# Where the positional product and the next step's value product stand in TensorE's queue: a fused attention and routed-expert block on one Trainium2 core

## What is computed

```python
h = _layernorm(x) * (1 + ca) + sa
q, k, v = jnp.einsum('bsx,xAnh->Abnsh', h, w)
a = jnp.einsum('bnqh,bnkh->bnqk', q + q_bias, k) * h ** (-0.5)
emb = jnp.einsum('sf,fnh->nsh', sins, positional * FREQS ** (-0.5))
a = a + relative_causal(jnp.einsum('bnqh,nvh->bnqv', q, emb) * h ** (-0.5))
a = softmax(where(mask, a, NEG_INF));  o = einsum(a, v);  x = x + ga * (o @ out_kernel + out_bias)
h = _layernorm(x) * (1 + cb) + sb
idx = argmax(softmax(h @ Wg + bg));  x = x + gb * gate * expert[idx](h)   # first 256 tokens of each expert
```

## Time and profile before

| what | value |
|---|---|
| median of three runs | 934.0 us |
| the profiled execution: its own time, its span | 934.63 us, 932.6 us |
| PE busy | 869.1 us, 93% of the span, 5515 matmuls |
| weight loads (PEld) | 684.8 us, 73% |
| DVE busy | 702.9 us, 75% |
| ACT busy | 704.5 us, 76% |
| POOL busy | 519.2 us, 56% |
| mean granted TensorE clock | 0.988 of full speed |

### The profile page before, as it was taken

The page is one execution under the profiler, slowest core; times in us unless marked ns, Lnnn a source line. Parts: engine busy times, 40 slices in busy tenths (PEclk is TensorE's granted clock), DMA queues, the critical chain, the costliest instruction groups (busy, mean ns, idle before and its releaser), DMA issues.

```text
span 932.6 us, 18151 instructions
## 1 busy us (share of the span) xinstructions
PE 869.1 (93%) x5515; PEld 684.8 (73%) x5515; DVE 702.9 (75%) x2115; ACT 704.5 (76%) x1971; POOL 519.2 (56%) x789
## 2 busy tenths in 40 slices
PE   7899999999999999999999999999999999998994
PEld 5666777767777777777776777777777777666994
DVE  4878778787878788777878787878877777843784
ACT  4688888878888888888887888888888888760551
POOL 3364545666556655665556655675566545543354
PEclk8999999999999999999999999999999999999998
DMA  7332221122100101011101110010101110105671
GB/s 286 92 91 61 85 84 52 46 56 60 44 24 18 54 22 44 24 41 40 32 24 36 36 43 24 21 38 20 44 24 35 33 38 18 32 9 197 224 217 40
DMA packets 36512, 56.01 MB, mean 60 GB/s; under 512 B 7446, under 2 KB 21511, under 8 KB 36160
## 3 DMA queue, kind: packets, MB, share of 16 engines
q1 hardware_dynamic: 32624, 46.16, 17.3%
q0 software_dynamic: 3072, 5.94, 1.8%
q10 hardware_dynamic: 720, 2.75, 0.8%
HBM read 23.96 MB, written 16.82 MB: 44 GB/s over the span
## 4 chain that ended last, share of the span: by engine, by line
PE 87%; issue 5%; DVE 2%; ACT 2%; DMA 1%; POOL 1%; SPq 0%; DVEq 0%; POOLq 0%; ACTq 0%
PE bank L837 23%; PE bank L867 15%; PE bank L847 15%; PE bank L804 13%; PE bank L823 5%; PE bank L874 4%; PE bank L834 3%; PE bank L1059 2%; PE bank L1048 2%; PE bank L1012 2%; ACT prob L611 1%; DMA kx<-in_ktab 1%; PE bank L895 1%; DVE klo L1207 1%; DMA x<-xbuf 1%
## 5 line engine op out<-in xcount | busy, mean ns | idle before, releaser
L451 POOL TENSOR_SCALAR prob<-prob,rsum 128x128 f32<-128x128 f32 (+3 forms) x512 | 263.7, 533 | 290.1 <-DVE rsum L1180 284.4
L611 ACT ACTIVATE prob<-srow,nmax 128x512 f32<-128x512 f32 (+3 forms) x512 | 287.0, 562 | 140.5 <-DVE nmax L1168 140.0
L1168 DVE CUSTOM_DVE_ANT_0 srow<-bank,consts 128x512 f32<-128x512 f32 (+3 forms) x512 | 246.4, 484 | 92.4 <-issue 52.2
L847 PE MATMUL bank<-consts,prob 128*128 128x128 f32 x1280 | 204.2, 274 | 0.2 <-POOL prob L451 0.2
L847 PEld LDWEIGHTS bank<-consts,prob 128*128 128x128 f32 x1280 | 155.1, 141 | 28.2 <-ACT pt L620 7.5
L837 PE MATMUL bank<-khi,qhi 128*128 128x512 f32 (+2 forms) x384 | 151.7, 395 | 18.8 <-issue 16.3
L867 PE MATMUL bank<-pt,v 128*64 128x512 f32 (+3 forms) x1024 | 151.9, 438 | 12.8 <-issue 10.8
L620 ACT ACTIVATE pt<-bank 128x384 f32<-128x384 f32 x318 | 151.6, 494 | 1.1 <-PE bank L847 1.0
L444 POOL TENSOR_TENSOR qlo<-qx,qhi 128x384 fp32r<-128x384 f32 x128 | 129.4, 1011 | 31.3 <-ACT qhi L579 31.3
L867 PEld LDWEIGHTS bank<-pt,v 128*64 128x64 f32 x1024 | 76.0, 136 | 84.0 <-issue 64.3
L837 PE MATMUL bank<-khi,qlo 128*128 128x512 f32 (+2 forms) x384 | 130.2, 339 | 0.0
(11 more groups left out here) (193 smaller groups left out, 1467.9 us busy)
## 6 DMA issues: line engine op xcount, KB each, us to landing
qx<-g SPq DMA_DIRECT2D x252, 64.0 KB, 2.0
xbuf<-fill SPq DMA_DIRECT2D x16, 385.0 KB, 4.2
x<-xbuf SPq DMA_DIRECT2D x16, 385.0 KB, 3.7
raw<-in_w SPq DMA_DIRECT2D x16, 256.0 KB, 3.3
prob<-in_w SPq DMA_DIRECT2D x16, 256.0 KB, 4.4
out<-row SPq DMA_DIRECT2D x8, 256.0 KB, 2.7
x<-in_x SPq DMA_DIRECT2D x1, 1792.0 KB, 15.0
modb<-mod_rows SPq DMA_DIRECT2D x8, 192.0 KB, 3.6
```

The source lines that it names most:

```text
L451: end = gp.tensor_scalar(part, part, rsum[:, par, 4 * h + q:4 * h + q + 1], 1.0, ALU.mult, ALU.mult)
L611: act.activation(prob[:, par, h, QOFF[q]:QOFF[q] + P * (q + 1)], srow[:, k % 4, 0:P * (q + 1)], ACT.Exp, bias=nmax[:, par, k:k + 1], scale ...
L847: last = pe.transpose(out[:, n * P:(n + 1) * P], prob[:, par, h, QOFF[q] + k * P:QOFF[q] + (k + 1) * P], ident)
L1168: dve.tensor_tensor_reduce(out=srow[:, k % 4, 0:w], in0=scb[k % 2][:, 0:w], in1=mask[:, S - w:S], scale=-1.0, scalar=BIG, op0=ALU.add, op1 ...
```

## The change

TensorE: `project_g` moves from k 6, ahead of the last scores, to k 7, behind them and ahead of `weighted`. The value projection of even steps moves from their k 1 to k 7 of the odd step before, also ahead of `weighted`; its waits for `x2`, `hh` and `prx` move with it, now in steps 1, 3 and 5. Odd steps keep their own value projection at k 1 and so have two. The wait for `hld` goes from each projection to the few places that need it, and the wait for the low keys of head 1 at k 4 goes, since `project_q` at k 3 has waited for them.

ScalarE: `evac_v` follows (at the end of odd steps, ahead of `evac_o`), and `evac_k(j + 1, 0)` goes ahead of `high_q(j + 1, 0)`. `second` stays where it is.

VectorE: in even steps `low_k(j + 1, 0)` comes first and `evac_g` behind it, with `recip` between its halves. `low` goes from k 7 to k 6 of step 4, `residual2` from k 7 to k 6 of step 1, `choice` from step 4 to k 1 of step 5, `route` and `index` from step 5 to k 1 and k 2 of step 6.

```diff
@@ scalar: step
-                    if before and k == 1 and not (last and V_OF[a][0]):
+                    if k == 1 and a % 2 and not (last and V_OF[a][0]):
                         evac_v(j + 4, prb[1], *V_OF[a][1:])
...
                     if after and k == 5:
+                        evac_k(j + 1, 0)
                         high_q(j + 1, 0)
-                        evac_k(j + 1, 0)
...
                 if after:
                     evac_k(j + 1, 1)
+                if a % 2 and v_after(j) is not None:
+                    evac_v(j + 5, prb[1], *v_after(j))
                 if before:
                     evac_o(j - 1)
@@ tensor: scores
-                    pe.wait_ge(s["kl"], 2 * j + h + 1)
+                    if k == 0 or j == NJ - 1:
+                        pe.wait_ge(s["kl"], 2 * j + h + 1)
@@ tensor: step
-                    if before and k == 1 and not (last and V_OF[a][0]):
-                        if a % 2:
-                            pe.wait_ge(s["gq"], j + 3)
-                        else:
-                            pe.wait_ge(s["ve"], j + 3)
-                            if a and not first:
-                                pe.wait_ge(s[(None, "x2", "hh", "prx")[a // 2]], b)
+                    if k == 1 and a % 2 and not (last and V_OF[a][0]):
+                        pe.wait_ge(s["gq"], j + 3)
...
-                    if k == 6 and a % 2 == 0 and j + 2 < NJ:
-                        pe.wait_ge(s["ve"], j + 4 if before else 1)
+                    if k == 7 and a % 2 == 0 and j + 2 < NJ:
                         if a == 2 and not last:
                             pe.wait_ge(s["hn"], b + 2)
-                        if a == 4 and not first:
+                        elif a == 4 and not first:
                             pe.wait_ge(s["lge"], b)
+                        else:
+                            pe.wait_ge(s["ve"], j + 4)
                         project_g(j // 2 + 1)
+                    if k == 7 and a % 2 and v_after(j) is not None:
+                        if first or a == 7:
+                            pe.wait_ge(s["ve"], j + 4)
+                        else:
+                            pe.wait_ge(s[("x2", "hh", "prx")[a // 2]], b)
+                        project_v(prb[1], *v_after(j))
@@ vector
-                if (a, k) == (4, 7):
+                if (a, k) == (4, 6):
                     low(n)
-                if (a, k) == (1, 7):
+                if (a, k) == (1, 6):
                     residual2(b)
-                if (a, k) == (4, 6):
+                if (a, k) == (5, 1):
                     choice(b)
-                if (a, k) == (5, 6):
+                if (a, k) == (6, 1):
                     route(b)
-                if (a, k) == (5, 7):
+                if (a, k) == (6, 2):
                     index(b)
...
-                    if k in (6, 7) and a % 2 == 0 and j + 2 < NJ:
-                        evac_g(j // 2 + 1, k - 6)
...
                 if after:
                     low_k(j + 1, 0)
+                places = a % 2 == 0 and j + 2 < NJ
+                if places:
+                    evac_g(j // 2 + 1, 0)
                 recip(j, par, 1)
+                if places:
+                    evac_g(j // 2 + 1, 1)
```

More of the change, by code:

```diff
@@ L240, in qraw, with v_after @@
             return qx[:, j % 2, h, :]
+        def v_after(j):
+            b, a = divmod(j + 1, PAIRS)
+            return None if b == B or b == B - 1 and V_OF[a][0] else V_OF[a][1:]
         def g_batch(c):
@@ L800, in project @@
                 else:
-                    pe.wait_ge(s["hld"], 2 * (n + 1))
                     hi, lo = (t[:, n % 2, :] for t in (hhi, hlo))
@@ L809, in project_q @@
                 pe.wait_ge(s["kl"], 2 * j)
+                if (n, a) == (0, 5):
+                    pe.wait_ge(s["hld"], 2)
                 project(prb[0][:, :], whi[:, a, 0:P], wlo[:, a, 0:P], n, "qp")
@@ L815, in project_g @@
             def project_g(c):
+                if c % NG == 0 and c:
+                    pe.wait_ge(s["hld"], 2 * (g_batch(c) + 1))
                 project(prb[1][:, :], gwhi[:, c % NG, :], gwlo[:, c % NG, :], g_batch(c), "tp")
```

## The result

| | before | after |
|---|---|---|
| median of 4 runs, us | 933.6 (933.0 to 934.8) | 983.2 (981.1 to 985.9) |
| profiled execution, us | 934.6 | 981.1 |
| its span, us | 932.6 | 979.1 |
| PE busy, us (matmuls) | 869.1 (5515) | 900.7 (5515) |

The changed kernel takes 1.053 times as long, with an interval of 1.050 to 1.056. Between the two profiled executions the difference is 46.5 us, between the medians 49.6. The forecast was 976 us, its range 961 to 986: sign and range held, and the forecast was 7 us too low.

What follows compares the result with a forecast made beforehand. TensorE's idle time was taken to bound the kernel. Step terms of +4.8 us a batch made 34 over seven batches, +1 for the first: 934.6 to 969.6; the clock's +7.5 gave 977, forecast as 976 us, range 961 to 986.

Steps and rivals of the forecast that it cites:

- The wait for `hh`: Step 3, k 7: the value product waits for ScalarE's `second`; TensorE idles 3.2 us, next step +3.5 us later.
- The rival in which these reads end in time: Shared bank's two reads end before TensorE reaches k 7: 927 us, chance 0.04; with late low queries 938 us, 0.03.
- The wait for `x2`: Step 1, k 7: the value product waits for `residual2` on VectorE; +1.3 us, about 1.1 us of it idle.
- Keys ahead of queries: ScalarE: `evac_k` first makes low queries 0.64 us later against 0.31 slack; steps 7, 0, 1, 3 +0.37 us, step 6 +0.15.
- the rival in which the low queries come in time: GpSimd's spans or ScalarE's order leave low queries in time: 1.3 us a batch less, 960 to 967 us, chance 0.12.
- Even steps free: Even steps losing their value product, some 0.7 us, become no shorter: `project_q` at k 3 waits for low keys anyway.
- The "0.5 to 0.6 us" of waiting: Sign expected in the profile after: `project_q` in even steps waits 0.5 to 0.6 us for `low_k`.
- the clock: Step 3's idle gap brings 1.2 GHz back: 1.6 us a fall, in two thirds of seven batches, +7.5 us (0 to +11).
- The rival in which the clock stays: Same waits but no fall to 1.2 GHz, since TensorE was fully busy around the gap: 969 us, chance 0.30.
- `choice`, `route` and `index`: VectorE: moved to steps 5 and 6, they delay these; +0.44 us for step 5, +0.85 for step 6, low queries included.
- Step 4: `low_k` first removes 1.35 us of waiting ahead of step 5, and the late `project_q` goes too: -1.7 us a batch.
- The sum: All eight steps: +4.8 us a batch, 34 over batches 1 to 7, +1 for the first batch, together +35 without the clock.

Runs made afterwards that it cites:

- e2_fill: The changed kernel with twelve thrown-away matmuls put ahead of the wait for `hh` in step 3: 967.8 us, ratio 1.0358 to the kernel before.
- e11_kfirst: The kernel before with only `evac_k` put ahead of `high_q` on ScalarE: 949.7 us, ratio 1.0144.
- e3_qfirst: The changed kernel with `high_q` ahead of `evac_k` again on ScalarE: 975.2 us, ratio 1.0447 to the kernel before.
- e4_vector: The kernel before with only the new VectorE order: 921.1 us, ratio 0.9874.
- e8_alone: The kernel before with only the value product of step 4 moved to k 7 of step 3, behind the wait for `hh`: 972.8 us, ratio 1.0402.
- e7_keepall_qfirst: The changed kernel with all even steps' value products back at k 1 and `high_q` ahead of `evac_k` again: 925.8 us, ratio 0.9880 to the kernel before.

## Why the prediction was right, and where it was not

**The wait for `hh`.** Predicted 3.2 us idle and +3.5 a step; the trace shows 3.17, and `e2_fill`, where the clock stays, +3.57 (15.88 against 12.31). It came from two rows, ScalarE's end of `second` and TensorE's last scores. The rival in which these reads end in time needed 3.1 us less, and the wait of 3.17 us rules it out.

**The wait for `x2`.** +1.3 predicted, +1.39 measured; 1.1 us idle, in the place said.

**Keys ahead of queries.** The slack of 0.31 us was real: +0.37 predicted in steps 0 and 7, +0.42 and +0.39 measured, and 0.36 to 0.39 us of waiting for `ql`. In `e11_kfirst`, where nothing hides it, the eight steps add to 102.5 us against 100.7, and seven times 1.8 is 12.6 of its 13.5 us. So the rival in which the low queries come in time is out. Its price was added up wrongly, too: four times 0.37 and 0.2 are 1.7 us a batch, not 1.3; `e3_qfirst` shows 0.8.

**Even steps free.** Right: `project_q` waits 0.24 us for the low keys, 4.25 after the step's start (402.05 - 397.80), where 4.22 was predicted. The "0.5 to 0.6 us" of waiting that I named as its sign was too much: it was 0.23 or 0.24 in steps 0, 4 and 6 and 0.17 in step 2, and I had no row for it.

**Mis-sized: the clock, 7.5 us predicted and 15 measured.** That it would fall was right; the two factors were not. I gave it two thirds of seven batches, and it fell in all seven. And I took 1.6 us a fall, 4 us at 0.60, where the steps lost 1.6 us four times (17.46 - 15.88) and 2.7 three times (18.6 - 15.88), 14.5 in all. The rival in which the clock stays would have needed the 1.00 of `e2_fill`. The row of the start that I took it from ended at 20.00, and I did not look at the stretches behind (0.82 from 20.00 to 24.00, 0.75 from 24.00 to 28.00); the upper end, 11, was seven times 1.6 and so too low as well.

**Mis-sized: `choice`, `route` and `index`.** +0.44 and +0.85 predicted for steps 5 and 6, +0.10 and +0.29 measured, 0.9 us a batch and 6 us in all. The durations of the place they leave don't hold in the place they go to: `route` and `index` were counted at 1.37 us (1.57 less the score tile) and took 0.88 in the kernel after. Two instructions, before and then after, in all eight batches (min/median/max in ns):

```profile
L1295 DVE CAST sidx<-rsm x8: 170/741/751, 201.5 to 850.7; 128x4 uint32<-128x4 f32 x8
```

```profile
L1308 DVE CAST sidx<-rsm x8: 165/166/170, 213.2 to 896.9; 128x4 uint32<-128x4 f32 x8
```

```profile
L1267 DVE SCALAR_TENSOR_TENSOR lgt<-lgt,consts x8: 226/479/483, 187.6 to 847.5; 128x64 f32<-128x64 f32 x8
```

```profile
L1280 DVE SCALAR_TENSOR_TENSOR lgt<-lgt,consts x8: 209/211/224, 199.8 to 893.7; 128x64 f32<-128x64 f32 x8
```

The same cast of 128x4 takes 741 ns in one place and 166 in the other. What differs is GpSimd beside it. In the kernel before, the seven slow casts and the seven slow `lgt` rows all ran while GpSimd was at `low_q` (from 402.69 to 403.72 in one batch); the eighth of each, behind the last step, had GpSimd idle and took 0.17 and 0.23 us. In the kernel after and in `e4_vector` all 32 had GpSimd idle and were quick, and in `e8_alone`, which has the old order, 14 of 16 were slow again, all 14 beside `low_q`. The slow cast also ends with `low_q`, not at a duration of its own: in the seven batches before, its end comes 0.02 to 0.03 us behind the end of `low_q`, and where it began later (0.43 us into it instead of 0.29) it took 0.62 us instead of 0.74. VectorE before, beside `low_q`, and in the last batch; GpSimd after; VectorE after:

```profile
403.12 0.62 DVE L1295 CAST sidx<-rsm 128x4 uint32<-128x4 f32 x1
...
850.70 0.17 DVE L1295 CAST sidx<-rsm 128x4 uint32<-128x4 f32 x1
```

```profile
534.63 0.61 POOL L417 CAST hlo<-vlo 128x512 fp32r<-128x512 f32 x1
537.97 1.11 POOL L442 DMA_INDIRECT xbuf<-row,sidx  x1 [2.73 <-DVE row L1309]
```

```profile
536.63 0.17 DVE L1308 CAST sidx<-rsm 128x4 uint32<-128x4 f32 x1
```

The reading that fits all 64 of these instances is that the small instruction is held until GpSimd's is through. It is argued and not shown: no run moved GpSimd's instruction alone. The Trainium skill, "GPSIMD Engine Reference", section "Specifications", lists GpSimd's SBUF interfaces as shared with VectorE and names contention with VectorE instructions that have two SBUF inputs or run in a 2-port mode. The `lgt` rows, with two SBUF inputs, fit that; whether the cast, with one, runs in such a mode no run here shows.

**Step 4: -1.7 predicted, -1.38 measured.** The 1.35 us went, all of it. The 0.36 us of a late `project_q` that I added had been read in one batch, in which step 4 took 14.59 us; in the others it takes 14.22. And it did not go: in the same batch step 4 takes 13.21 us in the kernel after, against 12.84 in the others, and every other run has it there too. So the reason given, a late reciprocal behind `second`, was wrong: in both kinds of batch the reciprocal begins 0.75 or 0.76 us after the step's start, and VectorE takes the first score tile 1.07 us after it in one and 1.43 in the other. What makes that difference is open.

**The sum.** Without the clock +34 was predicted for batches 1 to 7, and +32 came: (1.0 + 3.57) x 7. For the rest +1 was predicted and about +0.4 came. So the clock is 7 us more and the other terms 3 less: the profiled execution was forecast at 977 and took 981.1 us. The other 3 of the 7 us of miss lie between one execution and the median: 0.6 was taken off 977 and another 0.5 by rounding, where the median of the kernel after lies 2.1 above its profiled execution.

## What to carry to other kernels

A product moved ahead of other work in an in-order queue takes its wait along, and everything behind it then waits: find when the last reader of its bank ends, from that reader's engine, and compare it with when the queue gets there, before you count what the move fills. When parts of a change pull in opposite directions, price and run them apart: here the VectorE order alone gave 11 to 12 us, and was hidden under 61 us of losses. And when a gap lies in the middle of dense matmuls, read the granted clock behind it until it is back at full, for the gap's cost was 23 us of waiting and 15 more of slow matmuls.

## What the runs showed of the hardware

- At the same gap of 3.17 us, at seven places of one execution, TensorE fell to 1.2 GHz every time, but lost 1.6 us in four and 2.7 us in three. In `e8_alone` and `e3_qfirst` it fell at fourteen more such gaps, and one of these steps was as long. The four long ones are those with 0.82 to 0.88 over the gap itself; the other 17 have 0.96 to 1.00 there. Gaps of 1.1 us (`x2`), 1.8 us and 1.95 us (first step of the kernel after) left it at 2.4 GHz.
- Matmuls thrown away ahead of a wait that can't be shortened made a kernel 15 us faster.
- A late start can cost more than the gap. In the profiled execution of `e7_keepall_qfirst` TensorE waited 3.74 us at the start for the low input values, against 1.45 in `e4_vector`, and then ran at 1.2 GHz:

```profile
15.50 0.47 PE L811 MATMUL bank<-vhi,fwhi 128*128 128x512 f32 x1 [3.74 <-DVE vlo L1140]
```

```profile
15.50:20.00 4.50, 4.50 (x31) 0.62 0.94 398
20.00:25.00 5.00, 3.35 (x11) 0.50 0.11 43
25.00:30.00 5.00, 5.00 (x33) 0.50 0.00 0
```

  Its step 1 began at 39.7 us, that of `e4_vector`, whose clock was at 1.00 over these stretches, at 34.4. Of these 5.3 us 2.1 are its own wait for the last value evacuation at k 7 of the first step. Its steps from there on were no longer. That is why the steps of kernels within 5 us of each other were compared here, and not only their whole times.
- VectorE's small instructions took 166 ns or up to 751 for one cast, and the slow ones were without exception those beside GpSimd's `low_q`, and ended with it.
